# Attention on a sorted edge list: five gathered tiles per window in the first three blocks, and the turns of three begin later

## What is computed

```
h      = x @ kernel
score  = exp(clip(leaky_relu(h[src] . a1 + h[dst] . a2), -2, 2))
out    = segment_sum(alpha * h[...]),  alpha = score / (segment_sum(score) + eps)
x      = layernorm(x + out)
msg    = relu(relu([x[row], x[col]] @ Wm1 + bm1) @ Wm2 + bm2) @ Wm3 + bm3
agg    = segment_mean(msg) over the destination
x      = layernorm(x + x + relu([x, agg] @ Wn1 + bn1) @ Wn2 + bn2)
```

## Time and profile before

| | |
|---|---|
| median of three runs | 2108.68 us |
| the profiled execution | 2116.28 us |
| its span in the trace | 2114.4 us |
| TensorE busy (granted clock, mean) | 81% (0.96) |
| VectorE / ScalarE / GpSimd busy | 75% / 62% / 55% |
| attention windows | from 41 to 642 us of the span |

### The profile page before, as it was taken

How to read it: one execution, slowest core, us unless ns; L and a number is a source line. 1 busy time by engine, 2 the same in 40 slices (tenths; PEclk the granted TensorE clock), 3 DMA queues, 4 the chain that set the end, 5 groups by cost and what they waited for, 6 DMA issues and landing times.

```text
span 2114.4 us, 52410 instructions
## 1 busy us (share of the span) xinstructions
PE 1711.5 (81%) x15382; PEld 1488.1 (70%) x15382; DVE 1595.5 (75%) x3352; ACT 1301.9 (62%) x2361; POOL 1166.0 (55%) x1198
## 2 busy tenths in 40 slices
PE   5788887887778768888888889888888888888887
PEld 3567776777676557777777778777777777777774
DVE  6999998888876657777767767767776777776677
ACT  6146777787886646666656655656565665665564
POOL 4045667676760265555555566555556555556640
PEclk9999999999997889999999999999999999999998
DMA  4034556676672443333333333333333333333331
GB/s 101 20 73 94 102 104 119 120 121 118 120 116 53 138 119 109 109 107 107 107 101 109 109 105 110 106 105 106 107 108 109 109 109 105 105 107 108 108 86 31
DMA packets 141999, 216.65 MB, mean 102 GB/s; under 512 B 27997, under 2 KB 96849, under 8 KB 141914
## 3 DMA queue, kind: packets, MB, share of 16 engines
q0 software_dynamic: 49632, 123.31, 22.6%
q1 hardware_dynamic: 89128, 90.73, 18.4%
q10 hardware_dynamic: 3154, 1.60, 0.4%
HBM read 166.19 MB, written 10.28 MB: 83 GB/s over the span
## 4 chain that ended last, share of the span: by engine, by line
PE 49%; issue 10%; another core or an unknown queue 2%; ACT 2%; DVE 1%; ACTq 0%; DMA 0%; SPq 0%; DVEq 0%
PE ps L1357 11%; PE ps L1363 10%; PE ps L1358 9%; PE ps L1337 8%; PE psA L1375 4%; PE ps L1332 4%; PE ps L1342 2%; ACT h_hi L1409 1%; PE ps L1093 0%; ACT h L1413 0%; DVE x L1174 0%; ACT h L1417 0%; PE ps L1101 0%; DVE stats L1183 0%
## 5 line engine op out<-in xcount | busy, mean ns | idle before, releaser
L1310 POOL DMA_INDIRECT ga<-table_a,idx x784 | 777.7, 992 | 540.0 <-PE ps L1363 184.4
L1413 ACT ACTIVATE h<-ps 128x512 bf16<-128x512 f32 x392 | 233.9, 597 | 488.5 <-PE ps L1363 295.8
L1357 PE MATMUL ps<-wm_hi,h_hi 128*128 128x256 f32 x1568 | 428.1, 303 | 99.0 <-issue 71.3
L1485 DVE SCALAR_TENSOR_TENSOR rest<-ps,h 128x512 f32<-128x512 f32 x392 | 269.3, 691 | 241.3 <-ACT h L1413 203.7
L1358 PE MATMUL ps<-wm_lo,h_hi 128*128 128x256 f32 x1568 | 404.1, 288 | 39.9 <-issue 39.8
L658 POOL DMA_INDIRECT head_n<-scr_eye,row_at x250 | 303.3, 1213 | 228.3 <-issue 223.2
L1357 PEld LDWEIGHTS ps<-wm_hi,h_hi 128*128 128x128 f32 x1568 | 302.3, 193 | 158.6 <-issue 107.2
L1358 PEld LDWEIGHTS ps<-wm_lo,h_hi 128*128 128x128 f32 x1568 | 303.0, 193 | 63.8 <-issue 63.5
L1363 PE MATMUL ps<-wm_hi,h_lo 128*128 128x256 f32 x1568 | 276.9, 288 | 54.9 <-issue 52.1
L1490 DVE TENSOR_TENSOR h<-rest,h 128x512 bf16<-128x512 f32 x392 | 269.3, 687 | 46.9 <-issue 26.7
L1479 DVE SCALAR_TENSOR_TENSOR h_lo<-ps,h_hi 128x512 fp32r<-128x512 f32 x392 | 262.8, 690 | 24.0 <-ACT h_hi L1409 13.5
(11 more groups left out here) (212 smaller groups left out, 2496.4 us busy)
## 6 DMA issues: line engine op xcount, KB each, us to landing
dstb<-scr_dst SPq DMA_DIRECT2D x196, 126.0 KB
cnt<-stage SPq DMA_DIRECT2D x125, 195.3 KB
cnt<-stage SPq DMA_DIRECT2D x125, 109.9 KB
ga<-table_a,idx POOLq DMA_INDIRECT x784
bw<-table_b SPq DMA_DIRECT2D x196, 63.0 KB
table_b<-cnt SPq DMA_DIRECT2D x12, 336.0 KB
head_n<-scr_eye,row_at POOLq DMA_INDIRECT x250
table_a<-upper SPq DMA_DIRECT2D x12, 224.0 KB
```

Of the source, the lines that this page charges most:

```text
L1310: pool.indirect_dma_start(ga[:, u, k, :], None, table_a, bass.IndirectOffsetOnAxis(ap=idx[:, u, k:k + 1], axis=0)).then_inc(gathered[u][k] ...
L1357: pe.matmul(ps2[q][:, t % 2, :], hi, w_hi[:, k, :], start=False, stop=True, skip_group_check=True)
L1485: dve.scalar_tensor_tensor(rest1[:, u % 2, 2 * q:2 * q + 2, :], ps2[q][:, :, :], 0.0, h2[0][:, u % 2, 2 * q:2 * q + 2, :], ALU.max, ALU.su ...
```

## The change

The number of gathered tiles becomes a pair: five in the windows of the first three blocks (windows 0 to 14), two in all others. In the dense windows the third, which ScalarE makes, is therefore the sixth tile of the window, and the turns of three begin at the seventh in place of the fourth. `head_m` gets a second part of three tiles, which a second `hot_rows` fills. The five or two gathers of a window count on one semaphore per head slot instead of one per gather, and TensorE waits once, for all of them, ahead of its first head matmul.

```diff
-GATHERED = 2
-HEAD = GATHERED + 1
 TPT = 3
+DENSE = 3
+GATHERED = (5, 2)
-KEYS = TILES + 6
+KEYS = TILES + 8
+def gathered_of(w):
+    return GATHERED[0 if w < DENSE * WPB else 1]
+def slot_gathers(w):
+    return sum(gathered_of(i) for i in range(w % HEADS, w + 1, HEADS))
...
-        head_m = sb("head_m", [P, HEADS, WME, HEAD], bf16)
-        head_n = sb("head_n", [P, HEADS, GATHERED, SWP // 2], bf16, 256)
+        head_m = sb("head_m", [P, HEADS, GATHERED[0] // TPT + 1, WME, TPT], bf16)
+        head_n = sb("head_n", [P, HEADS, GATHERED[0], SWP // 2], bf16, 256)
...
-        gathered = [[sem(f"row_in{i}_{k}") for k in range(GATHERED)] for i in range(HEADS)]
+        gathered = [sem(f"rows_in{i}") for i in range(HEADS)]
...
+                    HEAD = gathered_of((v + 1) * WPB + u) + 1
                     head(t, v, u, first)
                     eng.reg_mov(stop, end)
                     with eng.Fori(first + HEAD, stop, TPT) as n:
...
-                    for s in range(GATHERED):
+                    for s in range(gathered_of(w)):
                         pool.indirect_dma_start(head_n[:, w % HEADS, s, :], None, scr_eye,
...
-                for s in range(GATHERED):
-                    pe.wait_ge(gathered[w % HEADS][s], 16 * (w // HEADS) + 16)
+                pe.wait_ge(gathered[w % HEADS], 16 * slot_gathers(w))
+                for s in range(gathered_of(w)):
                     for k in range(2):
...
-                hot_rows(head_m[:, w % HEADS, :, :], first, v, u).then_inc(head_ready, 1)
+                parts = gathered_of(w) // TPT + 1
+                for part in range(parts):
+                    last = hot_rows(head_m[:, w % HEADS, part, :, :], first if part == 0 else first + part * TPT, v, u)
+                last.then_inc(head_ready, 1)
```

More of the change, by code:

```diff
@@ L443, in attention @@
         block_keys = sb("block_keys", [P, 2, KEYS], i16)
-        row_at = sb("row_at", [P, ROWS_AT, GATHERED], i32)
+        row_at = sb("row_at", [P, ROWS_AT, GATHERED[0]], i32)
         centre = sb("centre", [BLK, 1], fp32)
@@ L643, in rows_of @@
                 first = pool.snap(pool.snap(regs[u % WPB], min_val=0, max_val=PACK * TILES) >> 10, min_val=0, max_val=TILES - 1)
-                pool.tensor_copy(row_at[:, w % ROWS_AT, :], T.edge_keys[:, 1, bass.ds(first, GATHERED)]).then_inc(row_ready, 1)
+                pool.tensor_copy(row_at[:, w % ROWS_AT, 0:gathered_of(w)], T.edge_keys[:, 1, bass.ds(first, gathered_of(w))]).then_inc(row_ready, 1)
             pool.reg_load(regs[0:2], T.win_tab[0:1, 0:2])
@@ L656, in body @@
                     pool.sem_inc(pool_order, 1)
-                    for s in range(GATHERED):
+                    for s in range(gathered_of(w)):
                         pool.indirect_dma_start(head_n[:, w % HEADS, s, :], None, scr_eye,
-                                                bass.IndirectOffsetOnAxis(ap=row_at[:, w % ROWS_AT, s:s + 1], axis=0)).then_inc(gathered[w % HEADS][s], 16)
+                                                bass.IndirectOffsetOnAxis(ap=row_at[:, w % ROWS_AT, s:s + 1], axis=0)).then_inc(gathered[w % HEADS], 16)
                     if u == 0:
@@ L700, in head @@
                 pe.wait_ge(head_ready, t * (BPT * WPB) + w + 1)
-                for s in range(GATHERED):
-                    pe.wait_ge(gathered[w % HEADS][s], 16 * (w // HEADS) + 16)
+                pe.wait_ge(gathered[w % HEADS], 16 * slot_gathers(w))
+                for s in range(gathered_of(w)):
                     for k in range(2):
-                        last = pe.matmul(bank[0:WME, k, 0:HALF], head_m[:, w % HEADS, :, s], head_f8[:, w % HEADS, s, k * HALF:(k + 1) * HALF],
+                        last = pe.matmul(bank[0:WME, k, 0:HALF], head_m[:, w % HEADS, s // TPT, :, s % TPT], head_f8[:, w % HEADS, s, k * HALF:(k + 1) * HALF],
                                          start=(s == 0), stop=True, skip_group_check=True)
@@ L723, in after @@
                 pe.wait_ge(third_ready, t * (BPT * WPB) + w + 2)
+                s = gathered_of(w)
                 for k in range(2):
-                    last = pe.matmul(psC[w % 2][0:WME, k, 0:HALF], head_m[:, w % HEADS, :, GATHERED], third_n[:, w % HEADS, k * HALF:(k + 1) * HALF],
+                    last = pe.matmul(psC[w % 2][0:WME, k, 0:HALF], head_m[:, w % HEADS, s // TPT, :, s % TPT], third_n[:, w % HEADS, k * HALF:(k + 1) * HALF],
                                      start=False, stop=True, skip_group_check=True)
@@ L786, in _, with apart_of @@
             regs = [act.alloc_register(f"act_win{i}") for i in range(WPB)]
-            def apart_of(u, made):
-                third = act.snap(act.snap(regs[u], min_val=0, max_val=PACK * TILES) >> 10, min_val=0, max_val=TILES - 1) + GATHERED
+            def apart_of(u, made, w):
+                third = act.snap(act.snap(regs[u], min_val=0, max_val=PACK * TILES) >> 10, min_val=0, max_val=TILES - 1) + gathered_of(w)
                 act.wait_ge(third_ready, made + 1)
@@ L807, in _ @@
             for w in range(2):
-                apart_of(w, w)
+                apart_of(w, w, w)
                 third_hot(w, w)
@@ L824, in body @@
                     w = (v + 1) * WPB + u
-                    apart_of(u, made + u)
+                    apart_of(u, made + u, w + 2)
                     act.wait_ge(window_summed, t * (BPT * WPB) + w + 1 + HEADS)
```

## The result

The changed kernel is slower. Its median is 2146.4 us of four runs (2141.29 to 2150.04) against 2107.66 us of four runs of the kernel before; the ratio is 1.0181, with a 95% interval of 1.0157 to 1.0205, so 38.7 us are lost. The forecast was a gain of 6 us, with 2097.5 to 2111 as range.

A forecast was written before the change was run, and what follows sets the result against it. TensorE was taken to bound windows 0 to 3, VectorE 4 to 14. Start +3.8, savings -3.6 and -8.8 gave -8.6; GpSimd's limit left -6.4, small terms +0.4: 2108.68 - 6.0 = 2102.7 us, range 2097.5 to 2111.

The forecast's parts named there:

- What bounds the kernel: TensorE paces windows 0 to 3; VectorE is full in windows 4 to 14, 71.91 of 72 us; GpSimd no bound.
- the saving of VectorE and TensorE: Windows 1 to 4, paced by TensorE, save 3.6 us; windows 5 to 14, paced by VectorE, save 8.8 us.
- The start, +3.8: Window 0: TensorE's first head waits for all five gathers, costing 3.8 us; bounds +2.7 and +5.
- the small terms: Windows 0 to 14: 45 more gathers may lengthen VectorE's turns, +0.4 us; later merged waits, ScalarE, SBUF and DMA unpriced.
- GpSimd as bound: Gathers for windows 6 to 14 take 57.6 us plus 7 of stalls, allowing only -3.2 us at window 14's head.
- The sum 107 + 57.6 + 7: End of window 14's gathers: window 6's released at 107, nine windows 57.6 us, stalls 7; stated as 171.2.
- the tail that I took as 0.84: In the stall estimate: us by which a gather begun inside VectorE's long instruction ends after that instruction.
- 2.6 for the rest: Beyond the start: GpSimd's limit, partly recovered after window 14, turns -8.6 us into -6.4; small terms add 0.4.
- the slower one: GpSimd's queue binds from window 6 to well past 14, 8.5 us per dense window: +5.8 us, 2114.5; chance 0.1.
- Rival 4: To 180 us, gathers under way hold back VectorE's 10 long instructions, +4 us, in all -2; chance 0.05.
- the fifth rival: Slower: GpSimd's queue binds from window 6 to well past 14, +5.8 us, 2114.5; chance 0.1.
- "What would show": Signs included heads of windows 11 to 14 waiting for the DMA, window 14's head at 171 to 174.

The follow-up runs named there:

- e10: Changed kernel with five-tile heads but two gathers per window, the other three head tiles left out of the result, slower chip: 2101.45 us, 0.9940 against before.
- e2: Changed kernel with five-tile heads but two gathers per window, three head tiles left out of the result, faster chip: 1785.09 us, 0.9934 against before.
- e7: Changed kernel with five gathers in windows 1 to 4 only, two elsewhere: 2106.54 us, 1.0045 against the kernel before.
- e8: Changed kernel with five gathers in windows 1 to 4 only, those of windows 1 to 3 spaced two turns apart: 2096.75 us, 1.0004 against before.
- e5: Unchanged copy of the kernel before, on the second group's chip: 2102.29 us, a single run.
- e9: Changed kernel with two gathered tiles per window plus three spare gathers nobody waits for in windows 0 to 14, slower chip: 2159.33 us, 1.0223 against before.
- e4: Changed kernel with TensorE's 22 turns of window 0 as straight code instead of a loop, faster chip: 1800.49 us, 1.0020 against before.
- e11: Changed kernel with TensorE's 22 turns of window 0 as straight code instead of a loop, slower chip: 2145.07 us, 1.0146 against before.
- e1: Changed kernel with two gathered tiles per window plus three spare gathers nobody waits for in windows 0 to 14, faster chip: 1803.33 us, 1.0037 against before.

## Why the prediction was wrong

- **What bounds the kernel, and the saving of VectorE and TensorE**: right. Without the start the forecast had 3.6 + 8.8 = 12.4 us for them; e10 has window 14 at 166.3 (179.3 before, on the first chip) and the run is 11.2 us shorter; in e2 it is 12.4. The counts came out (row one-hots x205 and x140, column one-hots x615).
- **The start, +3.8**: right in place (head at 49.49, forecast 49 to 50), wrong as the whole price of window 0, which lost 14.1 us. That the other 10 us come from the gathers behind it is shown by e7 and e8. In both window 0 gathers only two tiles and its turns begin about as early as before (48.06 in e5, 48.56 in e7, 47.55 in e8). With more gathers back to back behind it, it ends at 92.4 (e7) against 81.8 (e5); with the same gathers spaced, at 78.8 (e8).
- **The step that failed** is in the small terms: "45 more gathers may lengthen the turns of VectorE beside them", bounds 0 and +2, +0.4 taken. I asked only what a gather does to an instruction of VectorE. What gathers back to back do is slow TensorE's own instructions and delay its increments, for which VectorE waits: in window 0 two pauses of TensorE together take 12.0 us with filled slots before it, and 45 gathers that nobody reads cost 47 us in the whole run (e9) where the term had 0.4. The row was there: the 1.64 us before 54.28, just behind the earlier trace rows. The "18 in 4.94" next to it is rightly a low clock (0.50 from 47 to 53 us), but the pause is not. Priced from it in proportion, a run of 20 gathers in place of 8 would have cost 2.5 us more in window 0 alone, over the bound of +2; the measured 12.0 are far more than in proportion.
- **GpSimd as bound**: where nothing pauses (e4), windows 6 to 14 took it 69.8 us for the nine (100.80 to 170.57), forecast 57.6 + 7 = 64.6, and the last gather ended at 170.57, forecast 171.2; but it had started 6 us sooner than I had put it. (The sum 107 + 57.6 + 7 gives 171.6, not 171.2, and the tail that I took as 0.84 is 0.82 in its row; nothing hangs on either.) The head of window 14 came at 174.47 (forecast 172.9), since the data took 3.9 us from the end of the gather and not 1.7. What was wrong is its worth: the gathers cost 15.4 us there (e4 less e2), where I had 3.8 for the start and 2.6 for the rest. So the change would most likely not have gained 6 us on that chip either; its own unaltered form was not run there.
- **The rivals**: the slower one had a chance of 0.1, with GpSimd's queue at 8.5 us a window. The sign was right, the mechanism was not: GpSimd in the changed kernel had idle time (47.74 of 72 us), and heads waited for gathers only once. Rival 4 had gathers hold back another engine, but it was VectorE's long instructions; what they held back was TensorE. That the time came out slower is therefore no success of the fifth rival.
- **"What would show"**: TensorE waiting for the DMA at the heads of 11 to 14 was not there; VectorE not full and TensorE's "issue" were, which none of my cases had.

Not settled: through what a gather reaches TensorE's instructions and increments, why ScalarE's and VectorE's are spared, how much of the loss behind window 0 is each of the two, what length of a run of gathers starts a pause, and the 14 us between medians and traces.

## What to carry to other kernels

Price an added GpSimd gather as a disturbance of TensorE, not only as time on GpSimd and the DMA queues: look in the profile for TensorE idle with "issue" and others idle with "remote" beside runs of gathers. A pause that is small now can grow more than in proportion (1.64 us beside 8 gathers, 12.0 beside 20). Ask of each pause whether the data that the engine needs lay ready; if so, a deeper ring, which was not tried, could not have shortened it. Spacing the gathers by the consumer's progress, with one constant wait each, kept a gain of 5.6 us here. Time such a change on more than one chip before believing a result of a per cent.

## What the runs showed of the hardware

- Beside gathers back to back TensorE's register and branch instructions take 0.69 to 0.73 us, 25 of them between 40 and 230 us of the changed kernel.
- Such gathers delay TensorE's increments from 0.02 to as much as 10 us and more (e11: 55.11 recorded at 66.41) in four of five comparisons; in the fifth, on another chip, beside as many gathers (e1), they ended at 53.42 and 54.77 and were recorded at 53.44 and 54.78.
- The cost goes with the number of gathers: spare ones of 32 rows of 640 bytes (1.0206) and of 128 rows of 128 bytes (1.0203) cost nearly what those of 128 rows of 640 do (1.0223, on another chip).
- TensorE's granted clock is 0.76 in the stretch 41 to 110 us of the changed kernel and 0.93 before. From 57 to 71 us it is 0.50, the lower of its two levels, with TensorE busy for 3.96 of these 14 us; before, from 57 to 75 us, it is 1.00 with 13.34 of 18 busy. One matmul of a turn takes 0.47 us at the lower level and 0.30 at the higher. I read the clock as a consequence of the pauses that adds to the loss; no run separates it.
- That other chip is 300 us faster as a whole, and nearly all of that lies in the message stage, which gathers 784 times: from the same matmul to the end 1081 us in e1, 1385 before. Where e1's chain of waits has no "issue", e9's has 9%. The page's line for the chain that ended last, e1 and then e9:

```profile
PE 57%; DVE 1%; issue 0%; ACT 0%; DMA 0%; POOL 0%; POOLq 0%; DVEq 0%
```

```profile
PE 49%; issue 9%; another core or an unknown queue 2%; ACT 2%; DVE 1%; ACTq 0%; DMA 0%; SPq 0%; DVEq 0%
```

That the gathers of that stage cause it there was not tried.
